# The gelu of the first square layer goes back into its PSUM bank, and the engines' order lists are redone

## The chip, the cores and the metric

One Trainium2 chip; the program runs on one of its cores. The number that counts is the device time of one execution in microseconds; where several executions are given it is their median. The engines of the core work side by side, each through its own queue of instructions in a fixed order, and wait for one another by semaphores: TensorE (PE, matmuls), VectorE (DVE), ScalarE (ACT), GpSimd (POOL) and SyncE (SP, which only starts transfers here).

## What is computed

Two layers over four sequences of 1024 positions and 256 features. Each layer adds to x the product of a mixer and a gate, both of the normalised x. In the first layer the mixer is a wavelet transform with linear attention, and the gate is a feed-forward network with ternary weights; in the second the mixer is a selective state recurrence with a feed-forward block, the gate a mixture of eight experts. The change lies in the first layer's gate:

```python
def _L0_ffn_ref(x, w1_w, w1_s, w2_w, w2_s, h1_w, h1_s, h2_w, h2_s, w3_w, w3_s):
    h = jax.nn.silu(_tlin(x, w1_w, w1_s)) * _tlin(x, w2_w, w2_s)      # 256 -> 1024
    h = jax.nn.gelu(_tlin(h, h1_w, h1_s), approximate=False)          # first square, 1024 -> 1024
    h = jax.nn.gelu(_tlin(h, h2_w, h2_s), approximate=False)          # second square, 1024 -> 1024
    return _tlin(h, w3_w, w3_s)                                       # 1024 -> 256
...
    x = x + s * g
```

Beside it runs the recurrence h = exp(d*A)*h + d*B*x, y = sum over 16 states of h*C, of the second layer.

## The kernel before

Features lie on the 128 partitions, positions along the free axis. A sequence ("row", `b`) is cut into two chunks of 512 positions (`c`). The feed-forward network of one chunk is 24 tasks per engine: `kind` 0 (tasks 0 to 7) the two input products, `kind` 1 (8 to 15) the first square layer, `kind` 2 (16 to 23) the second; `m` is the tile of 128 of the 1024 hidden features. The activations enter the square layers as a pair of half-precision tensors, a high part and what is left of it, the low part, so that each output tile takes 2 x 8 matmuls of 128 x 512. `ffn_half` on PE issues them in two halves of eight.

For a tile of the first square four instructions follow each other: PE fills a PSUM bank (L1451, L1473), ACT takes the gelu from the bank into `tf`, a float32 buffer in SBUF with two halves (L957), ACT copies it times 4 into the high part `g1p[:, 0, m]` (L983), and DVE makes the low part `g1p[:, 1, m]` as tf times 4 less the high part (L1989). Tiles go round over a spare bank and three others (L282): tile 0 in the spare, 1 and 4 and 7 in `psf[:, 0]`, 2 and 5 in `psf[:, 1]`, 3 and 6 in `psy[:, 1]`. PE may refill a bank when the gelu of the tile before has read it (wait on `g1_f`). A gelu may write its half of `tf` when the low part two tiles earlier has read it (wait on `g1_lo`). The second square does the same with ACT (L965, L988), POOL making the low parts (L750), and `project` (L1498) sums over its tiles. `kind` 0 ends in DVE's L1985, ACT's L977 and POOL's L745.

In the turn of a row, this network runs side by side with the recurrence of the row before. Per chunk that is 16 steps `n`: PE spreads B and C over the partitions (`spread_b` L1597, `spread_c` L1604), DVE makes the input (L2184), two scans (L2201) and the output (L2217), ACT the decays (L1085), POOL adds up (L772). Afterwards come the wavelets, the second layer's feed-forward block and the experts, all in the same turn. `opening` is the first row alone, `closing` the last row's second layer alone. The order of the calls in each engine's queue is written out by hand as long lists in `opening`, `turn` and `closing`, one set for each engine; this order is what the engines follow, whatever becomes ready first. DVE also carries `head_norm` (L2135, L2137), `head_z` (L2141) and `head_late` (L2170) in the same lists. SP starts the loads and stores.

Of the kernel before, what the change touches and what calls it, by code (L numbers as in the profile page):

```python
# [132 lines left out]
def build(nc, a):  # L133
    ctx = ExitStack()
    with ctx:  # L135
# [147 lines left out]
        second_square = (psf[:, 1], psy[:, 1]) + (psf[:, 0], psf[:, 1]) * 3  # L283

# [414 lines left out]
        def _(pool):  # L699
# [126 lines left out]
            def turn(row, last):  # L826

                ffn_task(row, 0, 0); ffn_task(row, 0, 1); ffn_task(row, 0, 2); ffn_task(row, 0, 3)
                state_sum(row - 1, 0, 0); ffn_task(row, 0, 4); state_sum(row - 1, 0, 1); ffn_task(row, 0, 5)
                ffn_task(row, 0, 6); ffn_task(row, 0, 7); state_sum(row - 1, 0, 2); state_sum(row - 1, 0, 3)  # L830
                state_sum(row - 1, 0, 4); state_sum(row - 1, 0, 5); state_sum(row - 1, 0, 6); state_sum(row - 1, 0, 7)
                state_sum(row - 1, 0, 8); state_sum(row - 1, 0, 9); ffn_task(row, 0, 16); ffn_task(row, 0, 17)
                state_sum(row - 1, 0, 10); ffn_task(row, 0, 18); state_sum(row - 1, 0, 11); state_sum(row - 1, 0, 12)
                ffn_task(row, 0, 19); ffn_task(row, 0, 20); l0_low(row, 1); state_sum(row - 1, 0, 13)
                ffn_task(row, 0, 21); ffn_task(row, 0, 22); head_product(row - 1); ffn_task(row, 0, 23)
                state_sum(row - 1, 0, 14); state_sum(row - 1, 0, 15); ffn_task(row, 1, 0); ffn_task(row, 1, 1)
                ffn_task(row, 1, 2); ffn_task(row, 1, 3); state_sum(row - 1, 1, 0); state_sum(row - 1, 1, 1)
                ffn_task(row, 1, 4); ffn_task(row, 1, 5); ffn_task(row, 1, 6); ffn_task(row, 1, 7)
                state_sum(row - 1, 1, 2); state_sum(row - 1, 1, 3); state_sum(row - 1, 1, 4); state_sum(row - 1, 1, 5)
                state_sum(row - 1, 1, 6); state_sum(row - 1, 1, 7); state_sum(row - 1, 1, 8); state_sum(row - 1, 1, 9)  # L840
                ffn_task(row, 1, 16); state_sum(row - 1, 1, 10); ffn_task(row, 1, 17); ffn_task(row, 1, 18)
                ffn_task(row, 1, 19); state_sum(row - 1, 1, 11); state_sum(row - 1, 1, 12); state_sum(row - 1, 1, 13)
                ffn_task(row, 1, 20); state_sum(row - 1, 1, 14); ffn_task(row, 1, 21); ffn_task(row, 1, 22)
                state_sum(row - 1, 1, 15); ffn_task(row, 1, 23); expert_product(row - 1, 0)
                expert_product(row - 1, 1); expert_product(row - 1, 2); expert_product(row - 1, 3)
                expert_low(row - 1, 0); expert_low(row - 1, 1); expert_low(row - 1, 2); expert_product(row - 1, 4)
                expert_product(row - 1, 5); expert_low(row - 1, 3); expert_low(row - 1, 4); expert_product(row - 1, 6)
                expert_product(row - 1, 7); expert_product(row - 1, 8); expert_low(row - 1, 5)
                expert_product(row - 1, 9); expert_low(row - 1, 6); expert_low(row - 1, 7); expert_low(row - 1, 8)
                expert_product(row - 1, 10); l0_product(row, 0, wave); l0_out(row, 0, wave); expert_low(row - 1, 9)  # L850
                expert_low(row - 1, 10); expert_product(row - 1, 11); expert_product(row - 1, 12)
                expert_product(row - 1, 13); expert_low(row - 1, 11); expert_low(row - 1, 12)
                expert_product(row - 1, 14); expert_low(row - 1, 13); expert_product(row - 1, 15)
                l0_product(row, 1, wave); l0_out(row, 1, wave); expert_low(row - 1, 14); expert_low(row - 1, 15)
                expert_product(row - 1, 16); expert_product(row - 1, 17); expert_product(row - 1, 18)
                expert_low(row - 1, 16); expert_low(row - 1, 17); expert_low(row - 1, 18); expert_product(row - 1, 19)
                expert_product(row - 1, 20); expert_product(row - 1, 21); expert_product(row - 1, 22)
                gated_out(row - 1, 0, 0); expert_out(row - 1, 0); expert_low(row - 1, 19); expert_low(row - 1, 20)
                expert_low(row - 1, 21); expert_product(row - 1, 23); expert_low(row - 1, 22)
                expert_product(row - 1, 24); expert_product(row - 1, 25); expert_low(row - 1, 23)  # L860
                expert_low(row - 1, 24); expert_product(row - 1, 26); expert_low(row - 1, 25)
                expert_product(row - 1, 27); expert_low(row - 1, 26); expert_low(row - 1, 27)
                expert_product(row - 1, 28); expert_product(row - 1, 29); expert_product(row - 1, 30)
                expert_product(row - 1, 31); expert_low(row - 1, 28); expert_low(row - 1, 29); expert_low(row - 1, 30)
                expert_low(row - 1, 31)
# [4 lines left out]
            def closing(b):  # L870

                state_sum(b, 0, 0); state_sum(b, 0, 1); state_sum(b, 0, 2); state_sum(b, 0, 3); state_sum(b, 0, 4)
                state_sum(b, 0, 5); state_sum(b, 0, 6); state_sum(b, 0, 7); expert_product(b, 0); expert_product(b, 1)
                state_sum(b, 0, 8); expert_low(b, 0); expert_product(b, 2); expert_product(b, 3); expert_low(b, 1)
# [5 lines left out]
                expert_low(b, 11); expert_product(b, 13); expert_low(b, 12); state_sum(b, 0, 14)  # L880
                expert_product(b, 14); expert_product(b, 15); expert_low(b, 13); state_sum(b, 0, 15)
                state_sum(b, 1, 0); expert_low(b, 14); expert_low(b, 15); state_sum(b, 1, 1); state_sum(b, 1, 2)
                state_sum(b, 1, 3); state_sum(b, 1, 4); state_sum(b, 1, 5); state_sum(b, 1, 6); state_sum(b, 1, 7)
                state_sum(b, 1, 8); state_sum(b, 1, 9); state_sum(b, 1, 10); state_sum(b, 1, 11); state_sum(b, 1, 12)
                state_sum(b, 1, 13); state_sum(b, 1, 14); state_sum(b, 1, 15); gated_out(b, 0, 3)
                expert_product(b, 16); expert_product(b, 17); expert_low(b, 16); expert_low(b, 17); expert_out(b, 0)
                expert_product(b, 18); expert_low(b, 18); expert_product(b, 19); expert_product(b, 20)
                expert_product(b, 21); expert_low(b, 19); expert_low(b, 20); expert_product(b, 22)
                expert_product(b, 23); expert_low(b, 21); expert_low(b, 22); expert_product(b, 24); expert_low(b, 23)
                expert_low(b, 24); expert_product(b, 25); expert_product(b, 26); expert_low(b, 25); expert_low(b, 26)  # L890
                expert_product(b, 27); expert_low(b, 27); expert_product(b, 28); expert_product(b, 29)
                expert_product(b, 30); expert_low(b, 28); expert_low(b, 29); expert_product(b, 31); expert_low(b, 30)
                expert_low(b, 31); gated_out(b, 1, 3); expert_out(b, 1)

            l0_low(0, 0)
            opening()
# [6 lines left out]
        def _(act):  # L903
# [27 lines left out]
            def ffn_task(b, c, task):  # L931
# [15 lines left out]
                elif kind == 1:  # L947
# [1633 lines left out]
```

## Time and profile before

| | us |
|---|---|
| median of three executions | 1729.47 (1724.97 to 1736.57) |
| the profiled execution | 1727.02 |
| its span in the trace | 1725.3 |
| PE busy | 1420.9, 82% |
| DVE busy | 1403.6, 81% |
| ACT busy | 1118.5, 65% |
| POOL busy | 984.5, 57% |

The span is what the trace covers, 1.7 us short of the execution's time. Busy time is time in which an instruction of that engine runs. In the trace's views an instruction is named by its line in the kernel, its engine and operation, then output <- inputs by the program's names. A row's turn takes some 400 us and repeats three times; the first 225 us are the opening, the last 325 the closing.

### The profile page before, as it was taken

Reading aid. Unit: us, or ns where it says so; the run is one execution under the profiler, and the core shown is the slowest. Engines: PE = TensorE matmul, PEld = TensorE weight load, DVE = VectorE, ACT = ScalarE, POOL = GpSimd, SP = SyncE. Lnnn points to the kernel's source line nnn. Section 1 sums busy time; section 2 is a strip of 40 time slices with the busy share of each in tenths; the row PEclk is TensorE's granted clock in tenths of the full one; section 3 lists DMA queues with packets and bytes.
Section 4 is the critical chain, followed back from the end, with each engine's and each line's share of the span. In section 5 each row is a group of like instructions: output and inputs, shape, how many; then the busy total and the mean of one; then the engine's idle time right before and its main releaser. Section 6 shows DMA issues by size and latency. Waiting matters only on the chain. (4 is left out here: it accounts for less than half of the span.)

```text
span 1725.3 us, 16460 instructions
## 1 busy us (share of the span) xinstructions
PE 1420.9 (82%) x5229; PEld 622.9 (36%) x5296; DVE 1403.6 (81%) x1736; ACT 1118.5 (65%) x1563; POOL 984.5 (57%) x616
## 2 busy tenths in 40 slices
PE   4989989898998879898998789888998763555787
PEld 1444434434443334443443334443443321111333
DVE  2673369999789979999889979989879978999964
ACT  3626678868537768868537768878546854565664
POOL 2143155766208975766307975766406964786675
PEclk8999999999999999999999999999999975686989
DMA  8001000000101000000100100000100300000000
GB/s 191 16 0 61 1 13 1 14 11 1 74 13 37 25 25 1 0 25 0 74 13 20 42 25 1 1 25 1 74 13 0 135 25 0 1 0 1 0 13 13
DMA packets 12600, 42.43 MB, mean 25 GB/s; under 512 B 1866, under 2 KB 1890, under 8 KB 10466
## 3 DMA queue, kind: packets, MB, share of 16 engines
q1 hardware_dynamic: 11698, 35.08, 5.6%
q0 software_dynamic: 816, 6.30, 1.7%
q8 instruction: 42, 0.69, 0.2%
q14 instruction: 44, 0.36, 0.1%
HBM read 38.23 MB, written 4.19 MB: 25 GB/s over the span
## 5 line engine op out<-in xcount | busy, mean ns | idle before, releaser
L772 POOL TENSOR_TENSOR gx<-gx,sy 128x1024 f32<-128x1024 f32 x120 | 293.6, 2447 | 51.3 <-DVE sy L2217 45.0
L795 POOL TENSOR_TENSOR gate<-gate,lin 128x512 f32<-128x512 f32 x120 | 153.0, 1289 | 257.5 <-DVE lin L2337 246.7
L1473 PE MATMUL psf<-g1p,h2w 128*128 128x512 f16 x768 | 178.4, 381 | 2.3 <-ACT tf L965 1.6
L2184 DVE TENSOR_TENSOR psu<-so,psu 128x1024 f32<-128x1024 f32 x128 | 156.7, 1224 | 20.6 <-PE psu L1597 10.6
L1085 ACT ACTIVATE da<-delta,aneg 128x512 f32<-128x512 f32 x256 | 163.9, 712 | 8.0 <-DVE st L2201 7.3
L750 POOL TENSOR_TENSOR g2p<-tf,g2p 128x512 fp32r<-128x512 f32 x64 | 93.8, 1473 | 117.2 <-ACT g2p L988 116.8
L2201 DVE TENSOR_TENSOR_SCAN st<-da,carry,psu 128x512 f32<-128x512 f32 x128 | 156.8, 1267 | 1.8
L2201 DVE TENSOR_TENSOR_SCAN st<-da,psu 128x512 f32<-128x512 f32 x128 | 149.1, 1207 | 1.5
L800 POOL TENSOR_TENSOR ap<-gate,ap 128x512 f16<-128x512 f32 x116 | 143.9, 1258 | 4.4 <-ACT ap L1186 3.7
L2217 DVE TENSOR_TENSOR sy<-st,psu 128x1024 f32<-128x1024 f32 x94 | 114.5, 1218 | 7.9 <-issue 3.5
L1473 PE MATMUL psf<-hp,h1w 128*128 128x512 f16 x512 | 117.4, 379 | 4.3 <-ACT tf L957 4.1
L1178 ACT ACTIVATE gate<-gate 128x512 f32<-128x512 f32 x128 | 76.9, 624 | 59.4 <-DVE gate L2326 59.1
L745 POOL TENSOR_TENSOR hp<-tf,hp 128x512 f16<-128x512 f32 x64 | 73.6, 1161 | 70.2 <-ACT hp L977 70.1
L1473 PEld LDWEIGHTS psf<-g1p,h2w 128*128 128x128 f16 x768 | 73.7, 98 | 95.7 <-issue 7.1
L1186 ACT ACTIVATE ap<-gate 128x512 f16<-128x512 f32 x116 | 70.3, 622 | 57.3 <-POOL gate L795 47.6
L1759 PE MATMUL psu<-ap,mw 128*128 128x512 f16 x384 | 96.7, 393 | 10.0 <-POOL ap L800 9.4
L1597 PE MATMUL psu<-bcs,sel 128*128 128x512 bf16 x109 | 45.4, 417 | 70.6 <-DVE st L2201 63.3
L1498 PE MATMUL psy<-g2p,w 128*128 128x512 f32 x256 | 83.8, 455 | 17.1 <-POOL g2p L750 17.1
L759 POOL TENSOR_TENSOR sy<-st,c_row 128x1024 f32<-128x1024 f32 x18 | 43.5, 2419 | 86.8 <-DVE st L2201 50.3
L1147 ACT ACTIVATE hff<-psy,pk 128x512 f32<-128x512 f32 x48 | 32.7, 687 | 86.9 <-PE psy L1643 61.1
L965 ACT ACTIVATE tf<-psf,s_g 128x512 f32<-128x512 f32 x56 | 38.2, 686 | 77.7 <-PE psf L1473 52.5
L1658 PE MATMUL psu<-hff,wf 128*128 128x512 f32 x192 | 88.4, 595 | 0.0
(395 smaller groups left out, 3383.7 us busy)
## 6 DMA issues: line engine op xcount, KB each, us to landing
mw<-in_mlp_w SPq DMA_DIRECT2D x3, 2048.0 KB, 8.2
xn<-in_x SPq DMA_DIRECT2D x8, 512.0 KB, 5.9
wf<-in_wf SPq DMA_DIRECT2D x4, 1024.0 KB, 4.7
xr<-in_x SPq DMA_DIRECT2D x8, 512.0 KB, 3.9
x<-gx SPq DMA_DIRECT2D x8, 512.0 KB, 3.8
out<-outc SPq DMA_DIRECT2D x8, 512.0 KB, 3.1
mw<-in_mlp_w SPq DMA_DIRECT2D x3, 1024.0 KB, 10.2
h1w<-in_h POOLq DMA_DIRECT2D x1, 2048.0 KB, 13.2
```

The costliest lines, as they stand in the source:

```text
L750: pool.tensor_tensor(g2p[:, m % 2, 1], tf[:, m % 2], g2p[:, m % 2, 0].bitcast(F32), ALU.subtract).then_inc(g2_lo.sem, 1)
L772: pool.tensor_tensor(out, chunk(gx, c), sy[:, n % 2], ALU.add).then_inc(y_acc.sem, 1)
L795: pool.tensor_tensor(gate[:, r % NG], gate[:, r % NG], lin_at(b, r)[:], ALU.mult)\
L800: pool.tensor_tensor(ap2_at(b, r)[:, 1], gate[:, r % NG], ap2_at(b, r)[:, 0], ALU.subtract)\
L1085: last = act.activation(da[:, n % 4, t], delta[c][:, t], ACT.Exp, scale=aneg[:, t, n:n + 1])
L1473: last = pe.matmul(banks[m], w[:, t, cols], src[:, half, t], start=(t == 0 and half == 0), stop=(t == KF - 1 and half == 1))
L1498: last = pe.matmul(psy[:, t], w3[:, m, t * P:(t + 1) * P], g2p[:, m % 2, part], start=(m == 0 and part == 0), stop=(m == KF - 1 and part = ...
L1658: last = pe.matmul(second_bank(b, c)[:, t], wf2[:, m, t * P:(t + 1) * P], hff_of(b)[:, m % 2], start=(m == 0), stop=(m == KF - 1))
L1759: last = pe.matmul(out[:, h], w[:, e, t, h * P:(h + 1) * P], ap2_at(b, r)[:, part], start=False, stop=(q == NQ - 1 and part == 1))
L2184: dve.tensor_tensor(input_banks(n), chunk(so, c), both(psu[:, row_bank(n)]), ALU.mult)\
L2201: dve.tensor_tensor_scan(st[:, n % 2, t], da[:, n % 4, t], banks[:, t], 0.0 if c == 0 else carry[:, t, n:n + 1], ALU.mult, ALU.add).then_i ...
L2217: dve.tensor_tensor(sy[:, n % 2], st[:, n % 2], both(psb[:, 1]), ALU.mult).then_inc(cy_done, 1)
```

## The change

For tiles 1 to 7 of the first square the gelu's output is its own PSUM bank, where the high copy and DVE's low part read it. Tile 0, whose bank is needed for another purpose, still goes through `tf`. With that the waits change: the gelu of tiles 1 to 7 waits only for its matmuls; PE refills a bank when the low part of the tile before is made (`g1_lo` in place of `g1_f`), the second square's first tiles too; the second square's first two gelus wait for the low part of tile 0 and for those of `kind` 0 in place of all eight low parts. The order lists of PE, DVE, ACT and POOL are put together anew: the same calls in `opening`, `turn` and `closing`, some of them moved by a few places. SP's list is the same. The core of the diff, and of the lists the part in which the first square of a turn's chunk 0 stands:

```diff
+        def first_out(m):
+
+            return tf[:, 0] if m == 0 else first_square[m]
...
                     if c == 0 and m == 0:
 
                         act.wait_ge(out_sent.sem, out_sent.at(b - 2, NC))
 
-                    if m < 2:
+                    if m == 0:
                         act.wait_ge(h_lo.sem, h_lo.at(b, c * KF + KF))
-                    else:
-                        act.wait_ge(g1_lo.sem, g1_lo.at(b, k - 1))
-                    act.activation(tf[:, m % 2], first_square[m], ACT.Gelu, scale=s_g1[:, m:m + 1])\
+                    act.activation(first_out(m), first_square[m], ACT.Gelu, scale=s_g1[:, m:m + 1])\
                         .then_inc(g1_f.sem, 1)
                 else:
                     act.wait_ge(g2_mm.sem, g2_mm.at(b, k + 1))
-                    if m < 2:
-                        act.wait_ge(g1_lo.sem, g1_lo.at(b, c * KF + KF))
+                    if m == 0:
+                        act.wait_ge(g1_lo.sem, g1_lo.at(b, c * KF + 1))
+                    elif m == 1:
+                        act.wait_ge(h_lo.sem, h_lo.at(b, c * KF + KF))
...
-                    act.activation(g1p[:, 0, m], tf[:, m % 2], ACT.Copy, scale=G_UP).then_inc(g1_hi.sem, 1)
+                    act.activation(g1p[:, 0, m], first_out(m), ACT.Copy, scale=G_UP).then_inc(g1_hi.sem, 1)
...
-                            pe.wait_ge(g1_f.sem, g1_f.at(b, c * KF + 6))
+                            pe.wait_ge(g1_lo.sem, g1_lo.at(b, c * KF + 6))
...
-                            pe.wait_ge(g1_f.sem, g1_f.at(b, c * KF + 7))
+                            pe.wait_ge(g1_lo.sem, g1_lo.at(b, c * KF + 7))
...
-                        pe.wait_ge(g1_f.sem, g1_f.at(b, k - 2))
+                        pe.wait_ge(g1_lo.sem, g1_lo.at(b, k - 2))
...
-                        pe.wait_ge(g1_f.sem, g1_f.at(b, c * KF + 8))
+                        pe.wait_ge(g1_lo.sem, g1_lo.at(b, c * KF + 8))
...
-                    dve.scalar_tensor_tensor(g1p[:, 1, m], tf[:, m % 2], G_UP, g1p[:, 0, m],
+                    dve.scalar_tensor_tensor(g1p[:, 1, m], first_out(m), G_UP, g1p[:, 0, m],
                                              ALU.mult, ALU.subtract).then_inc(g1_lo.sem, 1)
...
-                state_input(row - 1, 0, 4); state_scan(row - 1, 0, 4); ffn_task(row, 0, 8); head_center(row - 1, 1)
-                state_input(row - 1, 0, 5); state_scan(row - 1, 0, 5); state_output(row - 1, 0, 5); l0_center(row, 1)
-                ffn_task(row, 0, 9); ffn_task(row, 0, 10); state_input(row - 1, 0, 6); ffn_task(row, 0, 11)
-                state_scan(row - 1, 0, 6); state_input(row - 1, 0, 7); state_scan(row - 1, 0, 7)
-                state_output(row - 1, 0, 7); head_norm(row - 1, 1); ffn_task(row, 0, 12); state_input(row - 1, 0, 8)
...
```

DVE's new order from there is: input 4, scan 4, input 5, head_center, scan 5, task 8, output 5, tasks 9 and 10, l0_center, task 11, input 6, scan 6, input 7, scan 7, output 7, task 12, input 8, head_norm, task 13, scan 8, task 14, input 9, scan 9, task 15, output 9, head_z0, input 10, scan 10, head_z1. On PE the halves of tasks 14 to 16 stood as 14,0; 15,0; 16,0; 14,1; 15,1; 16,1 and stand as 14,0; 14,1; 15,0; 16,0; 15,1; 16,1 (each with spreads between them).

## Rows read from the trace of the kernel before

**Rows 1.** The page: span, then busy us, share of the span, instructions of each engine.

```profile
span 1725.3 us, 16460 instructions
...
PE 1420.9 (82%) x5229; PEld 622.9 (36%) x5296; DVE 1403.6 (81%) x1736; ACT 1118.5 (65%) x1563; POOL 984.5 (57%) x616
```

**Rows 2.** Busy time by stretch: start:end, length, busy us (instructions) of each engine, TensorE's clock, DMA.

```profile
0.00:225.00 225.00, 188.27 (x776) 87.20 (x776) 100.53 (x174) 117.42 (x156) 65.38 (x61) 0.97 0.20 52
225.00:446.00 221.00, 193.35 (x805) 88.82 (x818) 201.01 (x186) 166.72 (x244) 144.73 (x77) 0.98 0.03 12
...
623.00:845.00 222.00, 196.83 (x804) 89.44 (x815) 202.97 (x191) 164.02 (x237) 140.83 (x74) 0.98 0.06 24
...
1024.00:1244.00 220.00, 198.43 (x799) 90.07 (x810) 202.77 (x197) 160.10 (x230) 135.41 (x72) 0.98 0.07 25
...
1400.00:1725.30 325.30, 202.61 (x550) 76.28 (x560) 257.64 (x295) 184.14 (x256) 211.35 (x123) 0.77 0.02 7
```

**Rows 3.** The same stretches, L1989 alone: DVE's busy us and instructions, clock, DMA.

```profile
0.00:225.00 225.00, 11.54 (x16) 0.97 0.20 52
225.00:446.00 221.00, 19.44 (x16) 0.98 0.03 12
623.00:845.00 222.00, 19.45 (x16) 0.98 0.06 24
1024.00:1244.00 220.00, 19.46 (x16) 0.98 0.07 25
```

**Rows 4.** L1989's durations (min/median/max), and waits: us in total, times, longest.

```profile
L1989 DVE SCALAR_TENSOR_TENSOR g1p<-tf,g1p x64: 668/686/2846, 62.5 to 1193.7; 128x512 f16<-128x512 f32 x64
...
ACT tf L957 <- DVE g1p L1989: 22.9, 10, 5.6
...
DVE g1p L1989 <- ACT g1p L983: 15.9, 9, 6.4
```

**Rows 5.** Timeline of DVE and of POOL around 773 us: start, us, instruction.

```profile
773.30 4.93 DVE L1989 SCALAR_TENSOR_TENSOR g1p<-tf,g1p 128x512 f16<-128x512 f32 x2
...
772.58 5.11 POOL L772 TENSOR_TENSOR gx<-gx,sy 128x1024 f32<-128x1024 f32 x2
```

**Rows 6.** Groups of DVE by shape: busy us, mean ns of one, idle before.

```profile
L1985 DVE SCALAR_TENSOR_TENSOR tf<-psf,s_h,sa 128x512 f32<-128x512 f32 x32 | 23.8, 744 | 27.6 <-ACT sa L945 24.2 <-POOL hp L745 3.0
...
L2337 DVE SCALAR_TENSOR_TENSOR lin<-lin,lin_one,psf 128x512 f32<-128x512 f32 x96 | 70.0, 745 | 13.6 <-PE psf L1705 10.9 <-remote 1.8
...
L2170 DVE SCALAR_TENSOR_TENSOR gx<-so,pk,gx 128x512 f32<-128x512 f32 x8 | 18.8, 2390 | 0.0
```

**Rows 7.** Groups of ACT by shape, with one function switch among them.

```profile
L1085 ACT ACT_TABLE_LOAD x43 | 55.2, 1283 | 0.8
...
L983 ACT ACTIVATE g1p<-tf 128x512 f16<-128x512 f32 x64 | 38.7, 626 | 0.9
...
L957 ACT ACTIVATE tf<-psf,s_g 128x512 f32<-128x512 f32 x40 | 27.2, 680 | 17.5 <-DVE g1p L1989 9.7 <-PE psf L1473 7.8
...
L1095 ACT ACTIVATE c_row<-psu 128x512 f32<-128x512 f32 x18 | 10.6, 587 | 1.8 <-PE psu L1604 1.8
...
L1020 ACT ACTIVATE psf<-psf,eps 128x512 f32<-128x512 f32 x6 | 4.0, 662 | 0.1
...
L1022 ACT ACTIVATE psf<-psf 128x512 f32<-128x512 f32 x6 | 3.5, 582 | 0.1
```

**Rows 8.** What DVE waited for from 623 to 845 us: in total, times, longest.

```profile
DVE tf L1985 <- ACT sa L945: 4.9, 4, 2.0
DVE nrm L2226 <- PE psf L1363: 4.2, 1, 4.2
```

**Rows 9.** Timeline of PE (first half of tile 7) and of DVE (low part of tile 4).

```profile
675.11 1.89 PE L1473 MATMUL psf<-hp,h1w 128*128 128x512 f16 x8
...
679.24 1.49 DVE L1989 SCALAR_TENSOR_TENSOR g1p<-tf,g1p 128x512 f16<-128x512 f32 x1
```

**Rows 10.** What PE waited for from 623 to 845 us.

```profile
PE psu L1597 <- DVE st L2201: 5.7, 3, 3.1
```

More of the change, by code:

```diff
@@ L833, in turn @@
[L833 to L837, printed above, removed]
@@ L847, in turn @@
[L847 to L851, printed above, removed]
@@ L862, in turn @@
[L862 to L865, printed above, removed]
+                expert_product(row - 1, 1); expert_low(row - 1, 0); expert_product(row - 1, 2)
+                expert_product(row - 1, 3); expert_low(row - 1, 1); expert_low(row - 1, 2); expert_low(row - 1, 3)
@@ new lines, in turn @@
+                ffn_half(row, 0, 16, 0); l0_var(row, 1); spread_b(row - 1, 0, 9); ffn_half(row, 0, 15, 1)
+                ffn_half(row, 0, 16, 1); spread_c(row - 1, 0, 9); spread_b(row - 1, 0, 10); head_delta0(row - 1, 1)
+                ffn_half(row, 0, 17, 0); ffn_half(row, 0, 17, 1); head_delta1(row - 1, 1); spread_b(row - 1, 0, 11)
+                spread_c(row - 1, 0, 10); ffn_half(row, 0, 18, 0); ffn_half(row, 0, 18, 1); head_bc(row - 1, 1)
+                spread_b(row - 1, 0, 12); spread_c(row - 1, 0, 11); ffn_half(row, 0, 20, 0); ffn_half(row, 0, 19, 0)
@@ L1875, in turn @@
+                head_delta1(row, 0); expert_up(row - 1, 24, 0); head_bc(row, 0); expert_down(row - 1, 16)
+                expert_down(row - 1, 17); expert_spread(row - 1, 12, 0); expert_up(row - 1, 25, 0)
+                expert_up(row - 1, 26, 0); expert_up(row - 1, 27, 0); expert_down(row - 1, 18)
+                expert_down(row - 1, 19); expert_up(row - 1, 28, 0)
                 if not last:
                     l0_mean(row + 1, 0)
-                expert_spread(row - 1, 13, 0); expert_up(row - 1, 28, 0); expert_down(row - 1, 19)
@@ L2363, in turn @@
+                head_z0(0, 0); head_z1(0, 0); lb_scale(0, 1, wave0); head_parts(0, 0); head_softplus(0, 0)
+                head_late(0, 0)
             def turn(row, last):
@@ new lines, in turn @@
+                head_center(row - 1, 1); state_scan(row - 1, 0, 5); ffn_task(row, 0, 8); state_output(row - 1, 0, 5)
+                ffn_task(row, 0, 9); ffn_task(row, 0, 10); l0_center(row, 1); ffn_task(row, 0, 11)
+                state_input(row - 1, 0, 6); state_scan(row - 1, 0, 6); state_input(row - 1, 0, 7)
+                state_scan(row - 1, 0, 7); state_output(row - 1, 0, 7); ffn_task(row, 0, 12)
+                state_input(row - 1, 0, 8); head_norm(row - 1, 1); ffn_task(row, 0, 13); state_scan(row - 1, 0, 8)
@@ new lines, in turn @@
+                ffn_task(row, 0, 14); state_input(row - 1, 0, 9); state_scan(row - 1, 0, 9); ffn_task(row, 0, 15)
+                state_output(row - 1, 0, 9); head_z0(row - 1, 1); state_input(row - 1, 0, 10)
+                state_scan(row - 1, 0, 10); head_z1(row - 1, 1); l0_scale(row, 1); state_output(row - 1, 0, 10)
+                state_input(row - 1, 0, 11); state_scan(row - 1, 0, 11); state_output(row - 1, 0, 11)
+                state_input(row - 1, 0, 12); state_scan(row - 1, 0, 12); state_output(row - 1, 0, 12)
@@ L2422, in turn @@
-                expert_scale(row - 1, 18); expert_scale(row - 1, 19); head_norm(row, 0); expert_clip(row - 1, 20)
-                expert_sum(row - 1, 0); expert_scale(row - 1, 20); expert_clip(row - 1, 21); expert_scale(row - 1, 21)
-                head_z0(row, 0); expert_clip(row - 1, 22); expert_scale(row - 1, 22); head_z1(row, 0)
+                expert_scale(row - 1, 16); expert_scale(row - 1, 17); expert_scale(row - 1, 18)
+                expert_clip(row - 1, 19); head_norm(row, 0); expert_scale(row - 1, 19); expert_clip(row - 1, 20)
```

694 lines of the change are left out of this document (347 added, 347 removed).

## The prediction

> **What bounds the kernel now.** I read the page first, then busy time by stage, then the groups of the two busiest engines, then the waits. The page gives two candidates at nearly the same share, PE 82% and DVE 81% [rows 1]; an average over stages says no more. By stage the picture is sharper [rows 2]: in each of the three stretches in which a row's feed-forward network shares the core with the state recurrence of the row before (225 to 446, 623 to 845, 1024 to 1244 us), DVE works 201 to 203 us of 220 to 222, some 91%, PE 193 to 198 us. In the first 225 us DVE works only 100.5, PE 188.3: there the matmuls bound. In the last 325 us no feed-forward is left.
>
> The change touches one DVE instruction, the low part at L1989. It costs 11.54 us for 16 in the opening, but 19.44 to 19.46 us for 16 in each shared stretch [rows 3]. Its shortest is 668 ns, its median 686, its longest 2846 [rows 4]. So it has a plain price near 0.69 us and sometimes a surcharge of a whole other instruction. The timeline shows whose [rows 5]: two of them take 4.93 us from 773.30, while POOL runs two additions (L772) of 5.11 us from 772.58. DVE's end is 778.23, POOL's 777.69. Both engines then read SBUF, L1989 two operands of it (tf and the half copy).
>
> **The change part by part.**
>
> *Low parts.* For output tiles 1 to 7 of each chunk, L1989 reads the gelu in its PSUM bank, tile 0 stays in tf. That is 14 of 16 in each stretch. Rows of the same operation with one operand in PSUM and one in SBUF: L1985 745 ns, L2337 745 ns, over 128 instructions together, in stretches where POOL works all the time [rows 6]. I take 0.745. Per stretch that is 14 x 0.745 + 2 x 0.69 = 11.8 us instead of 19.45, so 7.6 us of DVE work gone, 23 us over three. Bounds: at 0.69 each it is 8.4 us a stretch (25 in all); from below, nothing is saved if the surcharge isn't due to the second SBUF operand. L2170, with two SBUF operands too, means 2390 ns for a 128x512 instruction [rows 6], over three times the 745 of the PSUM forms, so I take the saving. In the opening 14 go from 0.69 to 0.745: 0.8 us more.
>
> The Trainium skill says this as a rule (SBUF — State Buffer, Who interferes with whom): a DVE instruction with two SBUF inputs contends with a GpSimd instruction that reads SBUF, the loser is blocked for the other's whole instruction, and one with at most one SBUF input doesn't contend. By that rule the surcharge goes altogether; the trace agrees as far as 4.93 us beside 5.11 us goes.
>
> Another of its rules speaks against the edit (VectorE: DVE Perf Modes, The TRN2 errata): a PSUM source has a fixed part of 120 cycles where an SBUF source has 58. By that page's clock this is an estimated 65 ns each, 3.6 us over 56 instructions. The rows here differ by 59 ns (745 against 686), and that is in the sum already.
>
> *ScalarE.* The gelu writes PSUM, the half copy reads it. PSUM to PSUM takes 662 ns (L1020) or 582 (L1022), gelu to SBUF 680 now; a copy out of PSUM 587 (L1095), out of SBUF 626 [rows 7]. So 56 gelus become 18 to 98 ns shorter and 56 copies 39 ns, 3 to 8 us in all. ACT works 160 to 167 us of a stretch [rows 2]: cover for that is idle time, worth nothing by itself. If ACT were last, it would be those 3 to 8 us.
>
> *Waits taken away.* A gelu waited for the low part two tiles earlier, because tf has two halves: 22.9 us in ten waits [rows 4]. These go for the first square. For the second square, gelu 0 no longer waits for all eight low parts, only for the first. What comes next in that chain is PE's last matmul of the tile. Of DVE's own idle time 15.9 us in nine waits hang on the half copy ahead of L1989 [rows 4], and in the second stretch only 1.0 of them; there DVE waits 4.9 us for the silu and 4.2 for PE's mean, neither touched [rows 8].
>
> *Waits added.* A bank is free only after its low part, not after its gelu. The square has four banks, tile 4 reuses tile 1's, 5 tile 2's, 6 tile 3's, 7 tile 4's; the second square starts in tile 5's. Behind that wait on PE's queue stand the rest of the square and the row spreads (L1597, L1604), and DVE's inputs wait for those. With the old order it would cost: in the second stretch PE starts tile 7 at 675.11, while the low part of tile 4 runs from 679.24 to 680.73 [rows 9]. That is 5.6 us late, and I take it for each of the six chunks.
>
> *Order lists.* They hold the same calls, only moved. Those that answer this: on DVE in chunk 0 of a turn, low part 4 now stands ahead of head_norm (two instructions of 1.22 us) and low part 1 only one instruction later; on PE the first half of the second square (task 16) moves behind the second half of tile 6 and the first of tile 7. Following the durations of the same rows through the new lists by hand, tiles 4 to 7 wait for nothing but task 16, some 2 us for low part 5; PE then comes out about 1 us ahead by the end of head_bc, and DVE, which is 3.8 us ahead after the chunk's last low part (half of 7.6), gives back some 1.5 at head_z1, whose matmul isn't ready. So part of what DVE saves is taken back by PE. The lists of ACT also have one function switch less in each turn and two less in the closing, each 1.283 us [rows 7]: 6.4 us of ACT, behind its idle time. No DMA is moved past another: SP's list is untouched, and POOL's holds no transfer in the turns. In the closing only positions change; I take 0, with 3 us either way, since its DVE (257.6 of 325 us) gets neither less nor more to do.
>
> *Sum.* Each stretch: 7.6 us less DVE work, of which I let two thirds reach the end, 5 us. One third is lost where PE is late, as traced above (1.5 of 3.8 in chunk 0, taken a little lower for chunk 1, where fewer of the row's other steps lie between). Three stretches: -15. Opening: +0.8, and I leave the hold there at nothing: DVE is idle over half of it, so the low part is prompt; without that cover it would be up to 2 us. Together -14.2. The profiled execution has a span of 1725.3 us and 1.7 us around it, 1727.0 in all; so 1712.8. The median of the runs shown, 1729.5, lies 2.5 above it: 1715.3, rounded to 1715.
>
> **The rivals.**
>
> *A, all of it arrives, and more.* DVE is at 91% in the shared stretches, so what it doesn't do shortens them one for one: 3 x 7.6 to 8.4 = 23 to 25 us, and a few of ACT's 22.9 us of waits stood ahead of something. 1729.5 - 25 = 1704. For it: DVE's timeline is gapless over tens of microseconds. Against it: PE works 193 to 198 us in the same stretches, so only 4 to 5 us below what DVE would have left (about 194).
>
> *B, PE takes it all back.* PE's work with its fixed order bounds the stretch, DVE's saving becomes waiting for spreads and means. Time 1729.5, or 1727 to 1733. For it: 193 to 198 us of PE work. Against it: PE waits in turn for DVE, 5.7 us in three waits of the second stretch for the scans alone [rows 10].
>
> *C, slower: the held banks.* Mechanism: PE stands before tile 4 and tile 7 until the low part, which sits in DVE's queue behind scans. Price from above: 5.6 us a chunk, 34 us over six, less the 14 gained: +20, so 1749. It decides from 2.4 us per chunk on (14.2 over six); below that the time is under the old one. Against it: the new lists bring the low parts forward.
>
> *D, the surcharge moves.* The surcharge is another one than the second SBUF operand, L1989 keeps 1.2 us in the stretches; then DVE gains nothing, and the lists decide: 1729 give or take 8.
>
> **How the numbers follow.** Forecast 0.36, A 0.27, B 0.17, C 0.13, D 0.07. The forecast's own range is 1708 to 1722. The range for 8 in 10 reaches from just under A (1700, with the closing's 3 us) to between B and C: 1738. About 1% (17.3 us, so below 1712.2 and above 1746.8) is what a measurement of this kernel can tell. Faster by over 1%: nearly all of A, a third of the forecast, a bit of D, 0.40. Slower by over 1%: most of C and a little of D, 0.13. The rest, 0.47, is within 1%.
>
> **What would show it.** L1989 with PSUM as source at 0.73 to 0.75 us in every stretch, its longest under 0.8, its two remaining SBUF forms per stretch as now. DVE's busy time over the whole falls by 20 to 24 us. The waits of the first square's gelu for L1989 are gone. PE's waits for L1989 ahead of L1473 stay under 2.4 us a chunk. Each shared stretch is some 215 to 217 us long instead of 220 to 222; the expert stretches between and the closing keep their length within 3 us. The prediction is wrong if L1989 keeps its long cases, or if PE stands in the first square for over 2.4 us a chunk, or if DVE's idle time in the stretches grows by as much as its work falls.

## The result, and the profile after

| | before | after |
|---|---|---|
| median of 20 executions each, us | 1732.33 (1724.97 to 1736.57) | 1737.62 (1729.67 to 1742.68) |
| ratio to before | | 1.0034, 95% interval 1.0019 to 1.0050 |
| profiled span, us | 1725.3 | 1736.0 |

The kernel is some 6 us slower, not 14 us faster. The profiled execution of the kernel before (1727.0 us) lies 5.3 us under its median, that of the changed kernel (1737.7) at its median, so the traces show 10.7 us where the medians show 5.3. Its page (span; busy us, share and instructions of each engine) answers [rows 1]:

```profile
span 1736.0 us, 16397 instructions
...
PE 1435.7 (83%) x5226; PEld 625.4 (36%) x5296; DVE 1376.6 (79%) x1736; ACT 1108.9 (64%) x1558; POOL 972.5 (56%) x616
```

DVE works 27 us less, ACT 10 us less, and yet the span is 10.7 us longer; PE is busy 15 us more. The low part, now L1994 (duration min/median/max, first and last start), against [rows 4]:

```profile
L1994 DVE SCALAR_TENSOR_TENSOR g1p<-psf,g1p x40: 665/684/692, 72.5 to 1198.2; 128x512 f16<-128x512 f32 x40
L1994 DVE SCALAR_TENSOR_TENSOR g1p<-psy,g1p x16: 665/678/692, 76.7 to 1196.5; 128x512 f16<-128x512 f32 x16
L1994 DVE SCALAR_TENSOR_TENSOR g1p<-tf,g1p x8: 666/688/2674, 68.9 to 1170.2; 128x512 f16<-128x512 f32 x8
```

All 56 instructions with a PSUM operand end within 692 ns; only the eight that still read `tf` have a long case. In the three shared stretches the 16 low parts take 12.6 us instead of 19.45 [rows 3]:

```profile
225.00:446.00 221.00, 12.62 (x16) 0.96 0.02 8
623.00:845.00 222.00, 12.60 (x16) 0.97 0.05 19
```

The third stretch has 12.61. So the saving is there, and it is DVE's waits that grew. What PE waited for in the second stretch (in total, times, longest), and one line of DVE's waits over the whole span:

```profile
PE psf L1455 <- issue: 2.9, 1, 2.9
PE psy L1455 <- DVE g1p L1994: 2.8, 1, 2.8
...
PE psf L1477 <- DVE g1p L1994: 2.2, 1, 2.2
```

```profile
DVE psu L2189 <- PE psu L1601: 36.3, 21, 3.8
```

L1601 is the row spread on PE, L2189 the DVE product that needs it; before, the two had 10.6 us between them. PE's timeline of chunk 0 in the second turn, and POOL's and DVE's beside it (start, us, instruction, idle before), show what the first two PE waits are:

```profile
671.46 1.90 PE L1477 MATMUL psf<-hp,h1w 128*128 128x512 f16 x8 [2.18 <-DVE g1p L1994]
...
689.46 1.89 PE L1455 MATMUL psf<-g1p,h2w 128*128 128x512 f16 x8 [2.94 <-issue]
```

```profile
666.78 2.34 POOL L763 TENSOR_TENSOR sy<-st,c_row 128x1024 f32<-128x1024 f32 x1 [5.46 <-DVE st L2206]
667.01 2.66 DVE L1994 SCALAR_TENSOR_TENSOR g1p<-tf,g1p 128x512 f16<-128x512 f32 x1
669.59 1.21 DVE L2222 TENSOR_TENSOR sy<-st,psu 128x1024 f32<-128x1024 f32 x1
670.72 1.28 DVE L1994 SCALAR_TENSOR_TENSOR g1p<-psf,g1p 128x512 f16<-128x512 f32 x2
...
688.67 0.69 DVE L1994 SCALAR_TENSOR_TENSOR g1p<-psf,g1p 128x512 f16<-128x512 f32 x1
```

At 671.46 PE gets tile 4's bank the moment low part 1, the first of the two at 670.72, is done; at 689.46 it gets the second square's first bank the moment low part 5, of 688.67, is. That second wait is named "issue", but it ends with the low part. Chunk 0 of a turn holds 2.2 + 2.9 us of such waits; chunk 1 holds 2.8, for low part 6 and the second square's second bank. The same three stand in all three turns.

The low part of tile 0, which still goes through `tf`, stands shortly ahead of low part 1. It takes 2.66 us beside POOL's addition of 666.78. In the shared stretches of the kernel before it took 0.67, and with new storage in the old order (s1 below) 0.67 too. Its new place in DVE's list sets it against POOL in chunk 0 of all three turns (2.66 to 2.67 us), and that is 2 us more ahead of low part 1, nearly as much as PE's first wait. No run took this place back alone, so what it costs is not shown.

**Where the 10.7 us are.** I cut each turn by the starts of four instructions in the timelines: the turn's first scan (L2206), the first scan of chunk 1, the last scan, and the second sum of the experts (L2349). Before, the pieces were 110.4, 92.7 and 183.3 us in the first turn. Differences to before, in us, over the three turns, then their sum:

| kernel | opening | chunk 0 | chunk 1 | behind it (experts) | closing |
|---|---|---|---|---|---|
| after | -0.8 | +8.2 +1.3 +4.0 = +13.5 | -2.4 -3.8 -3.3 = -9.5 | +4.1 +4.2 +2.4 = +10.7 | -1.0 |

The rest, -2.2, lies between turns. The opening is what comes before the first scan. Three effects, two of them not in the forecast: chunk 0 loses, chunk 1 gains, and the experts' part, of which the change touches only the order, loses.

### The profile page after: what moved, and what is told of

Read it like the earlier page. It is cut to its first block and busy times, and to the rows that moved or that the text cites. A ratio compares the mean times of both kernels' runs of the same rounds, so it can differ in the third digit from the quotient of the medians.

```text
span 1736.0 us, 16397 instructions
## 1 busy us (share of the span) xinstructions
PE 1435.7 (83%) x5226; PEld 625.4 (36%) x5296; DVE 1376.6 (79%) x1736; ACT 1108.9 (64%) x1558; POOL 972.5 (56%) x616
## 5 line engine op out<-in xcount | busy, mean ns | idle before, releaser
L776 POOL TENSOR_TENSOR gx<-gx,sy 128x1024 f32<-128x1024 f32 x120 | 286.4, 2387 | 62.2 <-DVE sy L2222 56.9
L799 POOL TENSOR_TENSOR gate<-gate,lin 128x512 f32<-128x512 f32 x120 | 156.6, 1323 | 277.6 <-DVE lin L2342 262.9
L2189 DVE TENSOR_TENSOR psu<-so,psu 128x1024 f32<-128x1024 f32 x128 | 156.7, 1224 | 52.2 <-PE psu L1601 36.3
L2206 DVE TENSOR_TENSOR_SCAN st<-da,carry,psu 128x512 f32<-128x512 f32 x128 | 156.8, 1267 | 2.5 <-ACT carry L1104 0.7
L754 POOL TENSOR_TENSOR g2p<-tf,g2p 128x512 fp32r<-128x512 f32 x64 | 88.3, 1384 | 123.1 <-ACT g2p L992 123.1
L2206 DVE TENSOR_TENSOR_SCAN st<-da,psu 128x512 f32<-128x512 f32 x128 | 149.1, 1206 | 5.4 <-DVE psu L2189 2.2
L1763 PE MATMUL psu<-ap,mw 128*128 128x512 f16 x384 | 101.0, 404 | 14.6 <-POOL ap L804 14.5
L1190 ACT ACTIVATE ap<-gate 128x512 f16<-128x512 f32 x116 | 69.9, 621 | 65.4 <-POOL gate L799 55.7
L1477 PEld LDWEIGHTS psf<-g1p,h2w 128*128 128x128 f16 x768 | 72.7, 98 | 92.7 <-issue 5.5
L1502 PE MATMUL psy<-g2p,w 128*128 128x512 f32 x256 | 82.8, 453 | 23.4 <-POOL g2p L754 23.1
L1662 PE MATMUL psu<-hff,wf 128*128 128x512 f32 x192 | 93.1, 614 | 0.0
L1601 PE MATMUL psu<-bcs,sel 128*128 128x512 bf16 x106 | 43.9, 414 | 55.0 <-DVE st L2206 53.2
L1647 PE MATMUL psy<-nrm,wf 128*128 128x512 f32 x192 | 87.3, 595 | 0.0
```

The source lines that it names most:

```text
L754: pool.tensor_tensor(g2p[:, m % 2, 1], tf[:, m % 2], g2p[:, m % 2, 0].bitcast(F32), ALU.subtract).then_inc(g2_lo.sem, 1)
L776: pool.tensor_tensor(out, chunk(gx, c), sy[:, n % 2], ALU.add).then_inc(y_acc.sem, 1)
L799: pool.tensor_tensor(gate[:, r % NG], gate[:, r % NG], lin_at(b, r)[:], ALU.mult)\
L1477: last = pe.matmul(banks[m], w[:, t, cols], src[:, half, t], start=(t == 0 and half == 0), stop=(t == KF - 1 and half == 1))
L1647: last = pe.matmul(first_bank(b, c, m), w[:, t, m * P:(m + 1) * P], nrm[c][:, t], start=(t == 0), stop=(t == KD - 1))
L1662: last = pe.matmul(second_bank(b, c)[:, t], wf2[:, m, t * P:(t + 1) * P], hff_of(b)[:, m % 2], start=(m == 0), stop=(m == KF - 1))
```

## The experiments

Medians are in us; a ratio is to the kernel before, measured beside it. The piecewise sums for all of them, as defined above:

| run | median | ratio, 95% interval | opening | chunk 0 | chunk 1 | experts | closing |
|---|---|---|---|---|---|---|---|
| s1 new storage, old lists | 1779.2 | 1.0291 (1.0263 to 1.0318) | +10.4 | +25.5 | +19.7 | -2.5 | -1.5 |
| s2 old storage, new lists | 1752.2 | 1.0132 (1.0107 to 1.0158) | +4.8 | +15.6 | +8.0 | +3.3 | -0.9 |
| s3 old storage, old lists, held banks | 1814.2 | 1.0490 (1.0464 to 1.0516) | +16.0 | +50.5 | +32.7 | -7.0 | -1.4 |
| s4 after, old lists behind the stretch | 1722.1 | 0.9954 (0.9938 to 0.9970) | -1.4 | +11.4 | -11.0 | -1.2 | -3.1 |
| s5 before, new lists there | 1734.8 | 1.0032 (1.0014 to 1.0051) | +6.1 | +0.3 | -1.0 | +7.3 | +0.4 |
| s6 s2 with held banks | 1765.6 | 1.0206 (1.0186 to 1.0227) | +6.4 | +26.4 | +2.4 | +9.0 | -1.2 |
| s7 s4 with chunk 0 as before | 1722.8 | 0.9951 (0.9928 to 0.9973) | +6.4 | +1.8 | -4.6 | -1.3 | -1.5 |
| s8 before, two groups moved | 1733.8 | 1.0013 (0.9996 to 1.0029) | +4.6 | +2.1 | +2.9 | -0.9 | -1.4 |
| s9 after, PE's expert list old | 1763.8 | 1.0182 (1.0153 to 1.0211) | +5.2 | +14.2 | -12.3 | +36.2 | -2.2 |
| s10 after, DVE's old | 1747.5 | 1.0084 (1.0055 to 1.0113) | -1.3 | +14.6 | -11.1 | +10.8 | -1.2 |
| s11 after, ACT's and POOL's old | 1731.0 | 0.9991 (0.9969 to 1.0014) | 0.0 | +14.6 | -12.3 | +5.6 | -1.5 |
| s12 s4 with the old closing | 1724.9 | 0.9969 (0.9947 to 0.9991) | -0.3 | +15.7 | -12.4 | -2.5 | -0.1 |
| s13 after, ACT's old | 1747.0 | 1.0106 (1.0064 to 1.0148) | -3.2 | +12.9 | -10.9 | +23.4 | -0.4 |
| s14 after, POOL's old | 1736.9 | 1.0030 (1.0008 to 1.0052) | -0.9 | +12.6 | -9.3 | +11.9 | -1.8 |
| s15 after, PE's and DVE's old | 1734.8 | 1.0027 (0.9997 to 1.0057) | -0.4 | +14.8 | -7.7 | +5.3 | -0.7 |

The pieces come from one execution each. s8, nearly the kernel before, shows how they scatter: single pieces from -2.3 to +2.4 us. The profiled execution of s10 is 10 us short of its median, so its pieces show too little; those of s5 and s7 are 4 to 5 us over theirs.

The opening scatters most. s5, s7 and s8 have the opening of before, line for line, and are 4.6 to 6.4 us longer in it in their traces. From 50 to 75 us TensorE's granted clock is 1.00 in the profiled execution of before and 0.86 in s8. Against these three the new opening is some 5 us shorter in eight of the nine kernels that have it with the new storage (all but s9). By this comparison the turns of the changed kernel lose more than the 5.3 us of the medians, and the opening gives some 5 back; no run changed the opening alone.

**Storage, lists and hold apart.**

> The gelu in its PSUM bank and all the new waits, but the order lists of before, with two groups of calls on PE moved so that nothing waits in a circle. Theory L (the new lists cost what the storage saves): 1717 to 1725 us, below the 1732 of before, since L1989 loses its surcharge of some 8 us a stretch and the lists' loss is gone. Theory H (the held banks eat the saving, lists or not): 1737 or more, PE's waits for the low part ahead of the first square 10 us or more above those of the changed kernel.

The old lists can't stand under the new waits as they are: PE would wait for a low part that DVE reaches only behind a spread that stands behind PE's wait. So two groups of PE's list are moved, in s1, s3 and s8:

```diff
-ffn_half(row, 1, 11, 0); spread_b(row - 1, 1, 5); ffn_half(row, 1, 12, 0); lf_average(row - 1, 0, True)
-spread_c(row - 1, 1, 5); spread_b(row - 1, 1, 6); ffn_half(row, 1, 11, 1)
+ffn_half(row, 1, 11, 0); spread_b(row - 1, 1, 5); spread_c(row - 1, 1, 5); spread_b(row - 1, 1, 6)
+ffn_half(row, 1, 11, 1); ffn_half(row, 1, 12, 0); lf_average(row - 1, 0, True)
...
-ffn_half(row, 1, 16, 0); ffn_half(row, 1, 16, 1); spread_c(row - 1, 1, 9)
-ffn_half(row, 1, 17, 0); spread_c(row - 1, 1, 10); spread_b(row - 1, 1, 10)
+ffn_half(row, 1, 16, 0); spread_c(row - 1, 1, 9); spread_b(row - 1, 1, 10)
+ffn_half(row, 1, 16, 1); ffn_half(row, 1, 17, 0); spread_c(row - 1, 1, 10)
```

> Before with nothing but the two groups of calls on PE moved, as in the runs with the old lists. It says what part of their 1779 and 1814 is owed to the move. If the hold is the cause there: 1729 to 1736. If the move itself costs: 1745 or more.

s8 is before with this edit alone, and it costs nothing that can be told. So s1's 49 us are not the move's: 1779 lies in theory H's range, and theory L alone, with 1717 to 1725, is out.

> Before, with tf, but PE refills a bank only after the low part (the hold without the saving), and the same two groups moved on PE as in the run with the old lists. Theory H: 1745 or more, as the surcharged low parts come late and PE stands. Theory L: within 6 us of before, 1727 to 1738.

s3 adds to s8 that PE's waits in the square are for `g1_lo` instead of `g1_f`; the gelu still goes through `tf`:

```diff
-                        pe.wait_ge(g1_f.sem, g1_f.at(b, k - 2))
+                        pe.wait_ge(g1_lo.sem, g1_lo.at(b, k - 2))
```

and likewise at the three waits for tiles of the second square. s3 is 80 us over s8. In the traces the six chunks of the turns are 78 us longer: with the old lists the hold costs 26 us a turn, 13 a chunk on average, more than twice the 5.6 the prediction priced. PE's waits in s3:

```profile
PE psf L2088 <- DVE g1p L3062: 39.6, 14, 5.5
PE psy L2066 <- DVE g1p L3062: 32.8, 7, 6.5
```

That is 72 us over eight chunks. At the same hold and the same lists, the storage gains 35 us (s3 to s1), with PE's two waits at 29.6 and 21.8 us instead. A low part that is no longer stretched to 2.8 us frees the bank earlier.

> The new order lists with tf as before, and the old waits (one more on PE ahead of the second square's third tile, which the new order needs). Theory L: slower than the changed kernel, 1742 to 1755, since the lists' loss stays and the surcharge on the low part is back. Theory H: no slower than before, 1727 to 1735, since no bank is held.

```diff
-                        pe.wait_ge(g1_f.sem, g1_f.at(b, c * KF + 8))
+                        pe.wait_ge(g1_lo.sem, g1_lo.at(b, c * KF + 8))
```

s2 has before's storage and waits (but for this one) and all the new lists. It is 22 us over before though no bank is held in the first square, which is what theory L had said. What DVE waited for there over the whole span:

```profile
DVE psu L3257 <- PE psu L2212: 26.1, 20, 4.3
```

These are the waits for row spreads, 10.6 us before and 36.3 after. So 15.5 of the 25.7 us by which they grew come with the lists alone.

> All new lists, tf as before, and PE refilling a bank only after the low part. Against the new lists with tf alone (1752.2) it is the price of the hold in lists made for it; against the changed kernel (1737.6) it is what PSUM storage gives at equal waits on PE. If the hold is what eats DVE's saving: 1760 to 1775. If the lists have hidden it: 1752 to 1758.

s6 adds the waits of s3 to s2. With 1765.6 us it lies in the range expected if the hold eats the saving. From before to s2, s6 and after: lists +22, hold +13, storage -28. By the pieces, where after's sums come from (us over three turns):

| step | chunk 0 | chunk 1 | experts |
|---|---|---|---|
| new lists (before to s2) | +15.6 | +8.0 | +3.3 |
| hold (s2 to s6) | +10.8 | -5.6 | +5.7 |
| storage (s6 to after) | -12.9 | -11.9 | +1.7 |
| sum | +13.5 | -9.5 | +10.7 |

The storage gives 25 us in the shared stretches, what the prediction called the whole saving. The lists take 24 of them back in the same stretches, the hold 5. In turn, the lists repair 42 of the 49 us that s1 lost. The likely reading is that they are made for the hold: PE's spreads and squares stand later, nearer to when the low parts are there, and that is paid also where nothing is held. Which moves in the lists cost the 24 us no run shows.

**Chunk 0.**

> PSUM storage and the new lists only for chunk 1 of each turn, tf and the old lists for chunk 0 and the opening, the old lists after the shared stretch, the new ones in the closing. In the run with the old expert part, chunk 0 from its first scan to chunk 1's first took 8.2, 1.5 and 1.7 us longer than before, chunk 1 from there to the last scan 2.5, 3.8 and 4.7 less, and the closing 3 less. If chunk 0 loses and chunk 1 gains on its own, this gives 1730 less 11 and 3: 1714 to 1719. If chunk 1's gain was only the delay of chunk 0 caught up: 1724 to 1730.

s7 puts the gelu into the banks only in chunk 1 of the turns; the opening and chunk 0 have before's lists, storage and waits, and so has the part behind the stretch:

```diff
+        def placed(b, c):
+
+            return b >= 1 and c == 1
+
+        def first_out(b, c, m):
+
+            return tf[:, m % 2] if m == 0 or not placed(b, c) else first_square[m]
```

The loss of chunk 0 is gone (+1.8 instead of +11.4 in s4), so it comes with the new lists, hold and storage of that chunk. But the kernel is no faster than s4, 1722.8 to 1722.1. Chunk 1 gains only 4.6 us where s4's gains 11, and s7 has the opening of before, 7.8 us longer in the traces than s4's. I had expected one of two values and got neither; I had left the opening out. Part of what chunk 1 gains may be what chunk 0 had left undone; the pieces don't add up freely.

**The part behind the stretch.**

> The changed kernel, with the turns' lists of before from the end of the shared stretch on (wavelets, second layer's feed-forward block, experts). Between the end of the shared stretch and the start of the next, the changed kernel is 4.5, 4.2 and 1.9 us behind before in its trace. Theory L, in the form that this part of the lists is to blame: 1724 to 1729, some 10 us below the changed kernel. Theory H: as the changed kernel, 1735 to 1739.

> Before in storage, waits and the lists of the shared stretches, opening and closing; only the part of the turns' lists after the shared stretch is the new one. If that part costs what its undoing gave back in the changed kernel (1737.6 to 1722.1, 15.5 us over three turns), 1742 to 1748. If the cost arises only together with the shifted arrivals from the PSUM version, 1730 to 1736.

s4 is after with the four lists of `turn` old from the end of the shared stretch to the turn's end; s5 is before with these parts new. DVE's lists differ in one more way than in places: its wavelet and choice steps are cut into other portions (`run(conv_steps, 14)` for 12), the same work in all. Of VectorE's list in s4, for one:

```diff
-run(conv_steps, 14)
+run(conv_steps, 12)
...
-expert_scale(row - 1, 3)
...
+block_out(row - 1, 1)
```

s4 is 15 us under after, and faster than before by 0.5%, with an interval that leaves out 1. In s5 the same lists cost 5.5 us by the ratio; I had expected 1742 to 1748, so most of that 15 again, and that was wrong. So this order costs time with either storage, and about three times as much behind the new stretch.

> The kernel after with one thing of before: TensorE's own list from the shared stretch to the end of the turn (expert products, means, head products); VectorE, ScalarE and GpSimd keep their new orders. Nothing is left out. The kernel after came out at 1737.6 us and the one with all four lists of that part old at 1722.1, so the part costs about 15. If TensorE's order is what costs it (it brings the expert's down products and the average products at other places, and TensorE is the busiest engine there): 1720 to 1727. If VectorE's order is: this stays at 1734 to 1741. If the price is that of lists that no longer fit together, a mixed kernel is slower than either: over 1741.

> The kernel after with VectorE's own list of before from the shared stretch to the end of the turn (the scaled and clipped halves, the conv steps, the choice between them); TensorE, ScalarE and GpSimd keep their new orders. Nothing is left out. If VectorE's order is what costs the 15 us of that part: 1720 to 1727. If TensorE's is: 1734 to 1741. If lists that do not fit together are the price: over 1741. If both must go back, each of the two kernels shows half, about 1730.

> The kernel after with ScalarE's and GpSimd's own lists of before from the shared stretch to the end of the turn; TensorE and VectorE keep their new orders. Nothing is left out. ScalarE's busy time in the three stretches is 316.4 us of 540 and the same with either list, so neither theory gives it a part in the price: 1734 to 1741, as the kernel after. Below 1730 would say that the places of the gelus, silus and copies of that part (the copy that comes late for a down product) are the cause.

> The kernel after with ScalarE's own list of before from the shared stretch to the end of the turn; the three other engines keep their new orders. Nothing is left out. s11, with ScalarE's and GpSimd's old, came out at 1731.0 us against 1737.6 for after. If ScalarE's order (silus and high copies of the experts in another alternation, lb_affine behind lb_square) carries the gain: 1729 to 1733. If GpSimd's order does: 1735 to 1740. If only the two together do: over 1738.

> The kernel after with GpSimd's own list of before from the shared stretch to the end of the turn; the others keep their new orders. Nothing is left out. If GpSimd's order (the low parts of the experts ahead of or behind their products) carries the 7 us of s11: 1729 to 1733. If ScalarE's does: 1735 to 1740. If only the two together do: over 1738.

> The kernel after with both TensorE's and VectorE's lists of before from the shared stretch to the end of the turn; ScalarE and GpSimd keep their new orders. Nothing is left out. Each of the two alone made the kernel slower (1763.8 and 1747.5 us). If the two lists fit each other and the rest of the 15 us is theirs: 1727 to 1733. If the lists of all four have to be of one making: over 1738.

Each is after with the named engines' lists of that part taken from before, ScalarE's for instance:

```diff
-hidden1(row - 1, 0, 2); expert_square(row - 1, 0); hidden1(row - 1, 0, 3); hidden_roots(row - 1)
-expert_square(row - 1, 1); q_expo(row, wave)
+expert_square(row - 1, 0); hidden1(row - 1, 0, 2); hidden1(row - 1, 0, 3); expert_square(row - 1, 1)
+hidden_roots(row - 1); q_expo(row, wave)
```

No single list carries the 15 us. PE's alone back costs 26 us more than after, DVE's 10, ACT's 9 by the medians (12 by the ratios, from four executions), POOL's nothing. ACT's and POOL's together (s11, between the two values expected) give back 7 us, PE's and DVE's 3 within their uncertainty, all four 15. I had given ACT's and POOL's lists no part because ACT's busy time is the same with either; that was wrong. In this part the lists work as a set, and a price can't be put down to one queue.

Part of what the set does is seen at PE. Behind the stretch, from the last scan to the second sum, after and s4 in the first turn: start:end, length, busy us (instructions) of PE, PEld, DVE, ACT, POOL, granted clock, DMA:

```profile
442.30:629.70 187.40, 162.44 (x535) 70.54 (x540) 156.83 (x253) 115.39 (x156) 101.77 (x75) 0.96 0.09 34
```

```profile
441.80:625.10 183.30, 159.18 (x535) 70.22 (x540) 155.75 (x254) 114.30 (x155) 100.28 (x75) 0.98 0.10 35
```

DVE, ACT and POOL work the same in both, within 1.5 us; PE is busy 3.3 us more for the same 535 matmuls. The clock accounts for it: it lacks 6.6 us of full speed after and 3.4 in s4. After, one microsecond at a time:

```profile
526.00:527.00 1.00, 0.00 (x0) 0.00 (x0) 1.00 (x1) 0.51 (x1) 0.46 (x1) 1.00 0.00 0
527.00:528.00 1.00, 0.81 (x2) 0.57 (x3) 0.96 (x4) 0.81 (x3) 0.28 (x1) 0.87 0.00 0
528.00:529.00 1.00, 1.00 (x2) 0.37 (x2) 1.00 (x2) 0.47 (x1) 1.00 (x2) 0.50 0.00 0
```

```profile
527.19 3.27 PE L1367 MATMUL psf<-y,meanw 128*128 128x512 f32 x4 [2.08 <-DVE zs L2110]
```

PE stands 2.08 us for a DVE result, then the granted clock is 0.50 (1.2 GHz), and four matmuls that take 1.88 to 1.96 us elsewhere take 3.27. In s4 the same mean stands where PE does not wait for it, and the clock stays at 1.00 from 525 to 533 us. Summed over windows of 2 us from 210 to 1400 us, the clock lacks 25.7 us of full speed before, 28.5 in s4, 29.0 in s11, 39.2 after, 42.9 in s9. Between s4 and after that is 10.7 us, beside a traced difference of 17.8. But the sum does not put the other kernels in order: s13 lacks 35.8, less than after, and its profiled execution is 9 us longer; s15 lacks 41.0, more than after, and its execution is 2 us shorter. So the clock can't be the whole of it. This is a reading of the traces: no run changed the clock by itself, so whether the low clock makes the loss or follows it isn't settled by an experiment.

**The closing.**

> The kernel s4_new_ffn_old_expert (new storage, new lists of the opening and the shared stretches, old lists behind them) with the four closing lists of before too. Nothing is left out. s4 came out at 1722.1 us, and from the last turn's end to the end of the span its trace is 3.1 us shorter than before's. If the new closing lists do that: 1724 to 1727. If it is only where the executions happened to lie, or follows from how the turn ends: 1720.5 to 1723.5.

s12 is s4 with `closing` of before in all four lists. It came out at 1724.9, in the range expected if the lists count, but with an interval that overlaps s4's. Its closing is 3 us longer in the trace. Over all runs, though, the closing shows no such gap: the kernels with the old one have -1.5 to +0.4 against before, those with the new one -3.1 to -0.4. That the new closing is worth 3 us is not shown.

## Why the prediction was wrong

By its own pieces, against the profile before (us over three turns): it had about -2.3 a turn in chunk 0, -2.7 in chunk 1, 0 behind and in the closing, +0.8 in the opening, together -14.2. The trace has +10.7, so 24.9 are to be found: chunk 0 13.5 + 6.9 = 20.4; experts 10.7; chunk 1 -9.5 + 8.1 = -1.4; opening, between the turns and closing -4.8. About 5 of the 24.9 go with the quick profiled execution of before, as the medians differ by only 5.3. By the medians of whole kernels the parts are storage -28, hold +13, lists +22; the prediction had them, together, at -14.2, with the lists at 0.

- *The mechanism of the saving: right.* L1994 with a PSUM operand takes at most 692 ns in all stretches, where L1989 took up to 2846 [rows 4]. The rule of the Trainium skill (SBUF — State Buffer, Who interferes with whom) says that a DVE instruction with at most one SBUF input, outside the 2-port modes, doesn't contend with GpSimd. The trace agrees, with no PSUM form over 692 ns and 12.6 us for 16 instead of 19.45.
- *Its size: 20.8 instead of 23 us* (69.9 to 49.1 over the kernel). The PSUM form is 0.683, not 0.745 us: the rows it was taken from write float32, this one half precision, and they don't show POOL working "all the time" (135 to 145 us of a shared stretch). But one of the two `tf` forms left in a stretch, tile 0's in chunk 0, now takes 2.66 us instead of 0.67, because the new list sets it against POOL: 12.61 - 14 x 0.683 leaves 3.0 us for the two, not 1.4. DVE's busy time fell by 27, of which these 20.8. The opening is 0.8 us shorter in the trace, not 0.8 longer, and some 5 shorter than in three other executions of the old one.
- *ScalarE: right.* The waits for the low part are gone, and nothing came of it: the gelu L959 now waits 36.2 us for PE's last matmul.
- *"Tiles 4 to 7 wait for nothing but task 16, some 2 us for low part 5": the step that failed first.* PE waits 2.2 us for tile 4's bank too and 2.9 for the other, 5.1 in chunk 0, and 2.8 in chunk 1. The prediction named 2.4 a chunk as the point from which the change loses; both chunks lie over it, though chunk 1 gains all the same, so that point itself was no good. I had traced the new lists from DVE's position before the change and let PE be 1 us ahead; a position carried by hand through four long queues didn't hold to 2 us here.
- *"Two thirds reach the end": failed with it.* DVE's idle time grew by 38 us while its work fell by 27. The largest part, 25.7 us, are waits for spreads on PE (10.6 to 36.3). s2, without the hold, already has 26.1 of these, so some 15 come with the new places in the lists and the rest with the banks. The second part is rival C's mechanism at a smaller size; chunk 1 did as forecast, -3.2 a turn against -2.7. There is a slip in the prediction's own case against rival A, too: it put PE 4 to 5 us below what DVE would have left. By its rows [rows 2] PE works 193 to 198 us and DVE would have had 193 to 195, so PE would have been level with it or above.
- *"Order lists: the same calls, only moved", priced at 0: failed, and the largest term.* With the storage unchanged they cost 22 us (s2), 24 of them in the shared stretches. And the experts' part, of which I looked only at lengths, took 10.7, though no instruction there changed its work.
- *Where rival C went wrong the other way:* it priced the hold with the old lists at 5.6 us a chunk from one pair of rows [rows 9]. s3 shows 13 on average. A late bank delays the spreads behind it, DVE waits for those, and the next low part is late again: that is how it reads in s3's waits, 37.3 us of DVE for spreads instead of 10.6.

For the change as a whole: storage gives 28 us in the new lists (s6 to after) and 35 in the old (s3 to s1); hold and new lists together take 33 (before to s6). With the old lists behind the stretch (s4) or also in chunk 0 (s7) it beats both kernels, by 8 us over before as the ratios have it. Chunk 0 is +8.2 in turn 1 against +1.3 in turn 2 with the same waits. About half of the 6.9 us between them goes with the clock: in turn 1 chunk 0 it lacks 3.4 us more than before, in turn 2 the same as before. Another 2.4 are there ahead of the first low part: by the third step turn 2 is 2.5 us ahead of before, turn 1 level. The eight matmuls behind the 2.2 us wait take 3.40 us in turn 1,

```profile
274.92 3.40 PE L1477 MATMUL psf<-hp,h1w 128*128 128x512 f16 x8 [2.20 <-DVE g1p L1994]
```

and 1.90 at 671.46 in turn 2, above. Why the clock fell the one time and not the other stays open, and so does what ties the four lists behind the stretch together.

## What to carry to other kernels

When an edit frees time on one engine by holding a buffer longer, price the hold first: find the instruction that frees the buffer, what stands queued behind the one that waits, and who waits for that; here the hold alone cost 80 us in the old order, where the saving gave 35, and 13 in an order made for it, where the saving gave 28, but that order cost 22 by itself. A reordering that comes with an edit is an edit of its own, in all stages it touches: run it with the old code, and the edit with the old order, before judging either. If all engines' lists were made as a set, change them as a set. Compare pieces of a trace with more than one execution of the old kernel: here its opening alone scattered by 6 us.

## What was not expected of the hardware

- The low part out of PSUM and SBUF takes 665 to 692 ns, as its form with two SBUF operands does undisturbed (668, [rows 4]); other DVE forms with a PSUM operand take 745 [rows 6]. The Trainium skill (VectorE: DVE Perf Modes, The TRN2 errata) gives a PSUM source the longer fixed part; in this instruction the trace doesn't show it.
- ScalarE from PSUM back into the same PSUM bank is no dearer than into SBUF. The gelu took 660 ns instead of 680, the copy out of PSUM 598 instead of 626 [rows 7]:

```profile
L959 ACT ACTIVATE psf<-psf,s_g 128x512 f32<-128x512 f32 x40 | 26.3, 660 | 36.4 <-PE psf L1477 36.2 <-PE psf L1455 0.2
...
L987 ACT ACTIVATE g1p<-psf 128x512 f16<-128x512 f32 x40 | 23.2, 598 | 0.3
```

- A wait of 2.2 us on PE cost close to twice that where the clock fell behind it: 1.89 us of matmuls became 3.40, with the granted clock at 0.50 for part of them. Behind the same wait in the next turn the clock stayed at 1.00 and they took 1.90.
